# Scores of the second attention layer are issued two tiles ahead of the row minimum

## What is computed

```python
h = (x - mu) * jax.lax.rsqrt(var + LN_EPS)
h = h * (1.0 + scale[:, None, :]) + shift[:, None, :]
q = (h @ Wq.T).reshape(B, T, N_HEADS, HEAD_DIM).transpose(0, 2, 1, 3)     # 16 heads of 32
c_kv = h @ Wkd.T
k = (c_kv @ Wku.T) ...   # 4 key heads, v likewise; rotary embedding on q and k
mask = _sparse_mask(T)   # own block within 64 keys, and every 64th key before it
scores = jnp.einsum('bhtd,bhsd->bhts', q, k_exp) / jnp.sqrt(32)
scores = jnp.where(mask[None, None], -jnp.inf, scores)
attn = jax.nn.softmax(scores, axis=-1)
y = jnp.einsum('bhts,bhsd->bhtd', attn, v_exp)
out = y.transpose(0, 2, 1, 3).reshape(B, T, C) @ Wo.T
return x + out
```

## Time and profile before

| | |
|---|---|
| time, median of 3 runs | 2933.84 us (2933.4 to 2935.29) |
| the profiled execution | 2936.59 us, its span 2934.8 us |
| PE busy over the span | 2468.2 us (84%) |
| DVE, ACT, POOL busy | 1624.5, 1207.7, 907.7 us |
| L1's attention, first to last score | 1243.8 to 1650.4 us |
| scores, minima and exponentials in L1 | 256 each |

### The profile page before, as it was taken

How to read it: one execution, slowest core, us unless ns; L and a number is a source line. 1 busy time by engine, 2 the same in 40 slices (tenths; PEclk the granted TensorE clock), 3 DMA queues, 4 the chain that set the end, 5 groups by cost and what they waited for, 6 DMA issues and landing times. The chain is left out here.

```text
span 2934.8 us, 48110 instructions
## 1 busy us (share of the span) xinstructions
PE 2468.2 (84%) x15828; PEld 2016.5 (69%) x15828; DVE 1624.5 (55%) x4635; ACT 1207.7 (41%) x2980; POOL 907.7 (31%) x982
## 2 busy tenths in 40 slices
PE   5879789798589999688788758889789999996786
PEld 4767677677468888576656547767568888885565
DVE  2677766677664343465575466576453333333876
ACT  1565565556441111365665546555431111112442
POOL 0133333233366676232232213233211212120422
PEclk8899889799889999768778779989989999997898
DMA  5000000000200000100000000000100000001000
GB/s 205 23 1 2 9 2 9 1 2 9 75 27 18 26 29 0 70 30 1 2 1 1 2 33 1 1 0 1 44 22 22 35 31 21 0 0 47 1 29 29
DMA packets 15743, 63.12 MB, mean 22 GB/s; under 512 B 2588, under 2 KB 3356, under 8 KB 10548
## 3 DMA queue, kind: packets, MB, share of 16 engines
q1 hardware_dynamic: 15540, 60.59, 5.8%
HBM read 56.36 MB, written 4.23 MB: 21 GB/s over the span
## 5 line engine op out<-in xcount | busy, mean ns | idle before, releaser
L837 ACT ACTIVATE l0a_prob<-l0a_prob,l0a_nmin 128x512 f32<-128x512 f32 x256 | 185.7, 725 | 199.5 <-DVE l0a_nmin L1095 199.2
L1617 POOL TENSOR_TENSOR l2m_hidl<-l2m_hid,l2m_hidh 128x512 fp32r<-128x512 f32 x64 | 100.9, 1576 | 480.2 <-DVE l2m_hidh L1593 480.2
L1259 POOL TENSOR_TENSOR l0a_prob<-l0a_prob,l0a_rinv 128x512 f32<-128x512 f32 x64 | 66.6, 1040 | 533.1 <-DVE l0a_rinv L1102 533.1
L1485 ACT ACTIVATE l2m_gate<-l2m_psG 128x512 f32<-128x512 f32 x64 | 38.3, 598 | 452.0 <-PE l2m_psU L1426 452.0
L1588 DVE TENSOR_TENSOR l2m_hid<-l2m_gate,l2m_psU 128x512 f32<-128x512 f32 x64 | 44.0, 688 | 300.1 <-ACT l2m_gate L1485 300.1
L673 PE MATMUL l0a_psT<-res_ident,l0a_prob 128*128 128x128 f32 x1024 | 165.9, 287 | 11.8 <-ACT l0a_PT L847 11.7
L1095 DVE CUSTOM_DVE_ANT_0 l0a_prob<-l0a_psS,l0a_mask 128x512 f32<-128x512 f32 x256 | 173.2, 687 | 2.6 <-issue 1.6
L1636 POOL TENSOR_TENSOR res_X<-res_X,l0m_share 128x512 f32<-128x512 f32 x128 | 162.1, 1293 | 25.7 <-DVE l0m_share L1577 24.7
L535 PE MATMUL l0a_psA<-l0a_wh,l0a_hTh 128*128 128x128 f32 (+1 forms) x512 | 155.5, 304 | 11.2 <-DVE l0a_wl L1210 5.8
L651 PE MATMUL l0a_psS<-l0a_kT,l0a_qT 96*128 96x512 f32 x256 | 128.0, 502 | 43.2 <-DVE l0a_nmin L1095 28.3
L1489 ACT ACTIVATE l0m_hid<-l0m_psG,l0m_b1c 128x512 f32<-128x512 f32 x64 | 44.0, 690 | 287.5 <-PE l0m_psG L1426 284.3
(11 more groups left out here) (390 smaller groups left out, 7875.3 us busy)
## 6 DMA issues: line engine op xcount, KB each, us to landing
l2m_stage<-in_l2m_w SPq DMA_DIRECT2D x8, 1536.0 KB, 6.6
l0m_stage<-in_l0m_w SPq DMA_DIRECT2D x8, 1024.0 KB, 4.8
cond_w<-in_wmod SPq DMA_DIRECT2D x6, 1024.0 KB, 5.9
res_X<-in_x SPq DMA_DIRECT2D x4, 1024.0 KB, 11.9
l0a_prob<-in_l0a_w SPq DMA_DIRECT2D x4, 1024.0 KB, 6.6
l1a_wmod<-in_wmod SPq DMA_DIRECT2D x4, 1024.0 KB, 5.4
out<-res_X SPq DMA_DIRECT2D x4, 1024.0 KB, 4.3
l_stage<-in_l_w SPq DMA_DIRECT2D x3, 1024.0 KB, 7.2
```

Of the source, the lines that this page charges most:

```text
L837: act.activation(prob[:, n % NP, 0:w], src[:, 0:w], ACT.Exp, bias=nmin[:, n % NP:n % NP + 1], scale=-1.0, accum_out=ssum[:, n % NP:n % NP ...
L1259: op = pool.tensor_tensor(x, x, r.to_broadcast([P, w]), ALU.mult)
L1617: pool.tensor_tensor(hidl[:, s % 2, m, :], hid[:, m, :], f32(hidh[:, s % 2, m, :]), ALU.subtract).then_inc(hl_done, 1)
```

## The change

In L1 the number of tiles that the scores run ahead of the step goes from one to two. L0 had two before and keeps it, L2 has one and keeps it. Nothing else is edited:

```diff
@@ -274,7 +274,7 @@
     HD = L.D
     NTILE = 4 * U
     LAG = 6
-    AHEAD = 2 if L is L0 else 1
+    AHEAD = 1 if L is L2 else 2
     NP = 8
     CL = 1
     PROJ0 = 0
```

## The result

The changed kernel takes 2945.7 us (median of 9 executions, 2940.17 to 2955.68), the kernel before 2933.4 on the same chip (9, 2921.21 to 2942.16): a ratio of 1.0046, 95% interval 1.0026 to 1.0066. The forecast was 2946. The profiled execution took 2949.67 with a span of 2947.9, 13.1 above that of before, where the sum said 13.0. As the stages and the experiments show, that agreement flatters the sum.

What follows compares the result with a forecast made beforehand. L1's attention was bound mostly by PE, busy 352 of 416 us, with DVE and ACT short by phase. Terms 5.1 + 6.7 + 0.9 + 0.3 gave 13.0 us, so 2933.84 became 2946.8, less 1: 2946, range 2933 to 2955.

Steps and rivals of the forecast that it cites:

- The place and the queue: L1's group boundaries: scores wait for query copies, PE holds the transposes behind them, and DVE's copy comes late by 1.8 us.
- Inside the groups, 0: Scores inside L1's groups wait for minima, but PE's later waits hide it: 0 us, between bounds of 0 and 11.
- Norm boundaries, 1.7 each: Group 1 to 2 with layer norm behind it, batches 0 to 2: 1.7 us each, 5.1 together.
- The foretold sign at PE's wait before the products: PE's wait of 4.00 us before the products ahead of the norm was to grow past 5.
- Six other boundaries, 1.14 and 1.0: Boundaries without norm or output projection: five at 1.14 us, the one where the batch loop jumps back 1.0; together 6.7.
- `proj` boundaries, 0.45 in two and nothing in batch 0: Group 2 to 3 with `proj` behind, batches 0 to 2: PE loses 0.45 us in batches 1 and 2; total 0.9.
- `out` boundaries, +0.1: Group 0 to 1 with `out` before, batches 1 to 3: DVE's idle takes most, 0.1 us each, 0.3 together.
- minus 1 for slack: 1 us taken off the median forecast of 2946.8, as a chain worked out at rigid distances has unseen slack.
- L1's stretch longer by some 12 us, all other stretches equal: Sign in the profile after: L1's attention stretch grows by some 12 us and no other stretch changes.
- hidden after all: Rival: PE's new boundary waits lie where ACT is full anyway; time stays 2934, or up to 2939; chance 0.20.
- The cross-check with L0: L0's scores wait 14.7 us for keys and queries, L1's 2.7; matching L0 would put 12.0 us more on PE.
- The rule of the Trainium skill (Perfetto Trace Analysis, Matmuls) on rotating through PSUM banks: Cited under the faster rival (2923, chance 0.10): using the third bank more would help, though no L1 score waited for banks.

Runs made afterwards that it cites:

- Both splits: Second layer two tiles ahead except each group's first four tiles, one ahead: 2930.9 us, ratio 1.0000; the reverse: 2948.61 us, ratio 1.0062.
- the reversed order: The changed kernel with each step's transposes issued ahead of its score in the second layer: 2928.55 us, ratio 0.9990 to the kernel before.
- the unchanged L1 with the long stretch: The kernel before with L0's first four tiles of each group one tile ahead, L1 unedited: 2944.39 us, ratio 1.0026; L1 took 418.1 us.

## Why the prediction came out right, and what in it was not

*The place and the queue* were right. The loss is at the boundaries between groups, it starts from a score that waits for a query copy, and it reaches DVE through the transposes that stand behind that score. Both splits and the reversed order show it, with the timelines.

*Inside the groups, 0*: right. Tiles with a lead of two there cost nothing, in spite of 14.3 us of waits for minima.

The costs by boundary that follow come from one profiled execution each. Where L1's program was unchanged, single boundaries still differed from the kernel before by -2.2 to +3.8 us with the clock, so they are rough.

*Norm boundaries, 1.7 each*: 1.7, 2.6 and 2.5, and batch 0 lost 3.3 more in steps 36 to 39, where the clock was 0.5 for longer than before. That can't be put down to the lead: the unchanged L1 with the long stretch lost 3.3 there too (tiles 36 to 44). The foretold sign at PE's wait before the products (from 4.00 to past 5) was wrong: it is 3.48, since PE came to it later by 4.1 us and the copy it waits for by 3.6. My lateness was also measured in durations of the upper level.

*Six other boundaries, 1.14 and 1.0*: 0.5 for the first; 2.5, 1.1 and 1.9 between batches; 2.6 and 2.3 in batch 3. My 6.7 was too low in sum (10.9). *`proj` boundaries, 0.45 in two and nothing in batch 0*: 0.1 and 0.3, and -1.5 in batch 0, where two kernels with an unchanged L1 have -2.1 and -2.2. *`out` boundaries, +0.1*: -0.5, -0.6 and -0.8. The kernel with lead 1 at group starts has -0.5, 0.0 and -1.9 there, so no gain of the lead is shown.

*The mis-sized step* is the one that I left out: the sum holds the granted clock of the kernel before fixed. By the line through the executions, the change costs 3.2 us at equal clock, or 4.7 with the mixture; with the flatter slope it is 5.9, or 7.0 with a mixture of 1.1. The other 7 to 9 go with the clock. So rigid distances, which gave 13, and "minus 1 for slack" were too high by a factor of two to three for the waits themselves, and a term that was never in the sum made it up. This division is an estimate, and the clock's cause is inferred. The foretold sign "L1's stretch longer by some 12 us, all other stretches equal" failed: 19.2, -3.5 and -2.6. The rival "hidden after all" (2934 to 2939) describes the executions at a clock near 0.89 nearly as well as my forecast does: the changed kernel's 2940.17 came at 0.889, where the kernel before takes 2935.7 (mean of 14 executions). So the number was right partly by luck.

*The cross-check with L0* (12.0 from its waits of 14.7) named the right waits, but not a price: in L0 a shorter lead took waits away and made the kernel slower.

*The rule of the Trainium skill (Perfetto Trace Analysis, Matmuls) on rotating through PSUM banks* gave nothing here: with the transposes first, a lead of two lets the scores run one bank further ahead, and the time is that of a lead of one (0.9990 and 0.9989).

## What to carry to other kernels

In an in-order queue, put the work that others wait for ahead of the instruction that reaches forward. In L1 a deeper lead cost nothing in that order, and in L0, which had the lead already, the reordering was worth 0.67%. A wait's price is what stands behind it in the queue, not its length: 14.3 us of waits for minima inside the groups cost nothing. And a producer that is moved earlier to end a wait can make a new one in the same queue. Before a sum is made at the durations of one profile, look at the granted clock over the stretch: a sum at fixed durations holds it fixed too.

## What the runs showed that I had not expected

For the same matmuls TensorE's granted clock in L1 was 0.78 at best (lead 1, transposes first) and 0.69 at worst (lead 2). An L1 whose program had not changed at all took 412.0 to 418.1 us, after edits in L0 alone. One kernel, with lead 1 at tiles 32 to 35 alone, went from 2932.88 to 2952.89 us between executions as its mean clock went from 0.891 to 0.882. For such a kernel one execution, or one profile, tells little of the median.
